# Per-category linear layer on one Trainium2 core: the categories taken in rotated order, their first weights and x loaded without the sort

## The reference

```python
selected_W = W[cat_ids]
selected_b = b[cat_ids]
x = x + jnp.einsum('bti,bio->bto', x, selected_W) + selected_b[:, None, :]
```

## Time and profile before

| what | value |
|---|---|
| three timed runs, median (lowest to highest) | 371.77 us (371.27 to 372.38) |
| profiled execution, first to last instruction | 371.0 us |
| PE busy | 356.9 us, 96% |
| POOL busy | 271.0 us, 73% |
| DVE, ACT busy | 172.1 us, 152.6 us |
| moved by DMA | 109.56 MB, mean 295 GB/s |

### The profile page before, as it was taken

One profiled execution on the slowest core, in us unless ns is written; L12 is line 12 of the kernel. 1 busy time (PEld: TensorE's weight loads), 2 busy tenths in 40 slices (PEclk: granted clock), 3 DMA queues, 4 the chain that ended last, 5 costly groups with the idle time before them and its releaser, 6 DMA issues.

```text
span 371.0 us, 6865 instructions
## 1 busy us (share of the span) xinstructions
PE 356.9 (96%) x1570; PEld 295.3 (80%) x1570; DVE 172.1 (46%) x271; ACT 152.6 (41%) x261; POOL 271.0 (73%) x145
## 2 busy tenths in 40 slices
PE   2969999999999999999999999999999999999996
PEld 2848888888888888888888888888888888888884
DVE  3534454454544545444454444545445454454542
ACT  4343245353544434343344525434542435453410
POOL 4299989678574688879893998989898889945000
PEclk9999999999999999999999999999999999999999
DMA  3979998999978799888998799989998999966622
GB/s 120 301 292 332 343 386 307 304 317 324 333 263 302 265 356 306 307 304 315 377 322 295 229 366 357 313 304 334 386 313 293 320 364 323 327 214 200 198 108 92
DMA packets 43379, 109.56 MB, mean 295 GB/s; under 512 B 4944, under 2 KB 5072, under 8 KB 38352
## 3 DMA queue, kind: packets, MB, share of 16 engines
q1 hardware_dynamic: 37296, 69.29, 52.7%
q0 software_dynamic: 5328, 38.80, 30.6%
q10 hardware_dynamic: 720, 1.05, 0.8%
HBM read 75.56 MB, written 33.55 MB: 294 GB/s over the span
## 4 chain that ended last, share of the span: by engine, by line
PE 92%; DMA 5%; DVE 1%; SPq 1%; issue 0%; DVEq 0%
PE pA L302 92%; DMA bb<-bias 4%; DMA idi<-ids 1%; SPq L132 0%; DVE os L275 0%; DVE xl L260 0%; PE pA L282 0%; SPq L117 0%; SPq L138 0%; DVE key L237 0%; DVE hot L241 0%; DVE cmp L239 0%; DVE rank L240 0%; DVE tb L244 0%; DVE idi L235 0%
## 5 line engine op out<-in xcount | busy, mean ns | idle before, releaser
L275 DVE TENSOR_TENSOR os<-pA,bb 128x512 f32<-128x512 f32 x128 | 88.7, 693 | 187.0 <-PE pA L302 178.7
L199 POOL TENSOR_TENSOR wl<-wr,wh 128x2048 fp32r<-128x2048 f32 x31 | 143.2, 4620 | 2.6
L302 PE MATMUL pA<-wh,xl 128*128 x512 | 137.7, 391 | 3.8 <-DVE xl L260 3.8
L302 PE MATMUL pA<-wl,xh 128*128 x512 | 137.7, 391 | 0.0
L302 PE MATMUL pA<-wh,xh 128*128 x512 | 137.1, 390 | 0.0
L219 ACT ACTIVATE pT<-xs 128x512 f32<-128x512 f32 x128 | 76.6, 598 | 110.9 <-DMA xs<-xt 105.1
L222 ACT ACTIVATE xh<-xs 128x512 fp32r<-128x512 f32 x128 | 80.4, 628 | 88.8 <-PE pA L302 88.4
L302 PEld LDWEIGHTS pA<-wh,xl 128*128 128x128 f32 x512 | 96.2, 188 | 24.3 <-issue 4.4
L302 PEld LDWEIGHTS pA<-wl,xh 128*128 128x128 f32 x512 | 96.7, 189 | 20.2
L302 PEld LDWEIGHTS pA<-wh,xh 128*128 128x128 f32 x512 | 96.4, 188 | 20.1
L195 POOL TENSOR_SCALAR wh<-wr 128x2048 fp32r<-128x2048 f32 x31 | 59.6, 1921 | 44.4 <-PE pA L302 38.6
(11 more groups left out here) (30 smaller groups left out, 14.1 us busy)
## 6 DMA issues: line engine op xcount, KB each, us to landing
xs<-xt SPq DMA_DIRECT2D x128, 256.0 KB, 5.4
out<-os SPq DMA_DIRECT2D x128, 256.0 KB, 4.9
wr<-w POOLq DMA_DIRECT2D x30, 1024.0 KB, 7.7
bb<-bias POOLq DMA_DIRECT2D x7, 1024.0 KB, 9.7
wr<-w ACTq DMA_DIRECT2D x4, 256.0 KB, 4.9
wr<-w SPq DMA_DIRECT2D x1, 1024.0 KB, 8.5
bb<-bias SPq DMA_DIRECT2D x1, 1024.0 KB, 13.1
idi<-ids SPq DMA_DIRECT2D x1, 64.0 KB, 3.8
```

The costliest lines, as they stand in the source:

```text
L199: eng.tensor_tensor(wl[:, at], wr[:, c % NR, :], wh[:, at].bitcast(f32), ALU.subtract).then_inc(s_w, 1)
L275: eng.tensor_tensor(os[:, i % NO, :], pA[i % NA][:, :], bb[:, bass.ds(at, D)], ALU.add).then_inc(s_fin, 1)
L302: mm = eng.matmul(pA[i % NA][:, :], xp[:, i % NH, k, :], wp[:, bass.ds(at + k * D, D)], start=(n == k == 0), stop=(n == 2 and k == KT - 1))
```

## The change

- **Order.** The categories are still taken in ascending order, but begin with that of element 0 and wrap around (`rot = (id - id[0]) & 31` in the sort key). Here the order becomes 21, 22, ..., 30, 31, 0, ..., 20, with 5, 5, 4, 3, 1, 5, 6, 2, 5, 6, 0, 6, 3, 9, 4, 3, 6, ... elements. So element 0 always comes first, and x of it is loaded at once, on ACT's queue.
- **First weights.** SP, ACT and POOL each read `ids[0]` from DRAM into a register (`category()`) and compute from it the address of every load of weights. SP issues the four chunks of c0, ACT issues c1 between its third and fourth conversion, POOL the rest.
- **Sort.** The ids come as one row on one partition; two matmuls spread it over the partitions and turn it into columns.
- **First batch elements.** PE works on element 0 chunk by chunk as the pieces of `wh`, `wl` come. c1 is prepared by ACT (`wh`), POOL and DVE (half of `wl` each).
- **Bias.** A group of four categories is read at the rotated place, from a bias array that the host writes twice in a row. The first row is loaded alone, the next three behind c1's identity step, and the other groups are issued by POOL in the middle of the preparation of their first category, where they stood beside the weights' load before.
- **End.** The last element's output is added and stored in two pieces, of 384 columns by SP and 128 by ACT.
- In ACT's and DVE's loops `xh` comes ahead of `pT`, the x load waits for `pT`, and PE waits for `xh` and `xl` apart.

```diff
+        def category(eng, name):
+            first = eng.alloc_register(f"{name}0")
+            eng.load(first, ids.rearrange("(a n) -> a n", a=1)[0:1, 0:1])
+            eng.reg_alu(first, first, C - 1, ALU.bitwise_and)
...
         @block.sync
-            eng.dma_start(idi[:, 0:128], ids.rearrange("(a n) -> a n", a=1).to_broadcast([128, 128])).then_inc(s_id, 16)
+            cat = category(eng, "sc")
+            c = cat(0)
+            for k in range(KT):
+                eng.dma_start(raw(0, k, k + 1), W[bass.ds(c, 1), :, k * D:(k + 1) * D].rearrange("a p d -> (a p) d"))\
+                   .then_inc(s_w0[k], 16)
             eng.wait_ge(s_tab, 1)
...
-                if i == 2:
-                    eng.dma_start(wr[:, 1, :], W[1, :, :]).then_inc(s_w1, 16)
-                if i == 3:
-                    bias_load(eng, 0)
...
         @block.gpsimd
-            def load(c):
-                eng.dma_start(wr[:, c % NR, :], W[c, :, :]).then_inc(s_wr[c % NR], 16)
-                if c % NB == 0:
-                    bias_load(eng, c // NB)
+            bias_load(eng, c0, 0, 1, s_b0)
+            eng.wait_ge(s_w1, 16)
+            eye = diagonal(1, 0, KT)
+            eng.tensor_tensor(eye, eye, ident[:, :, :], ALU.add).then_inc(s_ri, 1)
+            bias_load(eng, c0, 1, NB, s_bb[0])
+            eng.wait_ge(s_rh, KT)
+            eng.wait_ge(s_wd, 3)
+            eng.wait_ge(s_wp, 1)
+            load(2)
+            eng.wait_ge(s_rh, KT + 1)
+            eng.tensor_tensor(wl[:, chunk(1, 0, 2)], raw(1, 0, 2), wh[:, chunk(1, 0, 2)].bitcast(f32),
+                              ALU.subtract).then_inc(s_wp, 1)
+            eng.wait_ge(s_wp, 2)
+            eng.wait_ge(s_wd, 4)
+            eng.wait_ge(s_bb[0], 16)
+            eng.sem_inc(s_w, 1)
+            load(3)
+            for c in range(2, C):
+                eng.wait_ge(s_wr[c % NR], 16 * (c // NR))
+                eye = diagonal(c, 0, KT)
+                eng.tensor_tensor(eye, eye, ident[:, :, :], ALU.add).then_inc(s_ri, 1)
+                if c % NB == 0:
+                    bias_load(eng, c0, c, c + NB, s_bb[c // NB])
...
                 eng.tensor_scalar(wh[:, at], wr[:, c % NR, :], 1.0, 1.0, ALU.mult, ALU.mult).then_inc(s_wh, 1)
+                eng.wait_ge(s_wh, c - 1)
                 if c % NB == 0:
                     eng.wait_ge(s_bb[c // NB], 16)
...
         @block.scalar
+                if k == 2:
+                    eng.dma_start(wr[:, 1, :], W[bass.ds(cat(1), 1), :, :].rearrange("a p d -> (a p) d"))\
+                       .then_inc(s_w1, 16)
...
+                if i == 4:
+                    eng.wait_ge(s_ri, KT + 1)
+                    for k in range(0, KT, 2):
+                        eng.activation(wh[:, chunk(1, k, k + 2)], raw(1, k, k + 2), ACT.Copy).then_inc(s_rh, 1)
...
         @block.vector
+                for d0, d1 in ([(0, LAST), (LAST, D)] if i == B - 1 else [(0, D)]):
```

More of the change, by code:

```diff
@@ L173, in _ @@
                 eng.tensor_tensor(eye, eye, ident[:, 0:1, :], ALU.add).then_inc(s_ri, 1)
[L174 to L177, removed]
-            eng.sem_inc(s_w, 1)
[L179 to L185, removed]
+            eng.wait_ge(s_rh, 3)
@@ L243, in _ @@
             eng.wait_ge(s_bat, 1)
[L244 to L256, removed]
+            eng.tensor_copy(tb[:, :], pA[1][0:1, 0:128]).then_inc(s_tab, 1)
@@ L266, in _ @@
+            row = table(eng, "bo", tv, B, 0, (C - 1) * D)
             for i in range(B):
@@ L290, in _, with warm @@
-            eng.wait_ge(s_tab, 4)
-            eng.sem_inc(s_mm, 1)
-            row = table(eng, "wo", tc.rearrange("p n k -> p (n k)"), B, [1, 0], [C, (NW - 1) * KT * D])
-            for i in range(B):
-                c, at = row(i)
+            def warm(n):
+                for _ in range(n):
+                    eng.matmul(pA[0][:, 0:128], ones[:, :], ones[:, :], start=True, stop=True)
+            eng.wait_ge(s_one, 1)
+            eng.sem_inc(s_mm, 1)
+            warm(7)
+            eng.wait_ge(s_row, 2)
@@ new lines, in _ @@
+            warm(2)
+            HH, HL, LH = 0, 1, 2
+            first = [(HH, 0), (HH, 1), (LH, 0), (LH, 1), (HL, 0), (HH, 2), (LH, 2), (HL, 1),
+                     (HH, 3), (LH, 3), (HL, 2), (HL, 3)]
+            early = [(p, k) for p in (HH, HL, LH) for k in range(KT)]
+            plain = [(p, k) for p in (LH, HL, HH) for k in range(KT)]
+            pair = {HH: (xh, wh), HL: (xh, wl), LH: (xl, wh)}
+            eng.wait_ge(s_xh, 1)
+            for n, (p, k) in enumerate(first):
+                if p == HH:
+                    eng.wait_ge(s_rh, k + 1)
+                if (p, k) == (LH, 0):
+                    eng.wait_ge(s_xl, 1)
+                if p == HL and k == 2:
+                    eng.wait_ge(s_wp, 1)
+                elif p == HL:
+                    eng.wait_ge(s_wd, (1, 2, 0, 3)[k])
+                xp, wp = pair[p]
+                mm = eng.matmul(pA[0][:, :], xp[:, 0, k, :], wp[:, chunk(0, k, k + 1)],
+                                start=(n == 0), stop=(n == 3 * KT - 1))
@@ new lines, in _ @@
+            mm.then_inc(s_mm, 1)
+            eng.wait_ge(s_hot, 2)
+            eng.matmul(pS[0:1, 0:C], ones[:, 0:1], below[:, :], start=True, stop=True).then_inc(s_bat, 1)
+            eng.wait_ge(s_tab, 2)
+            row = table(eng, "wo", tc, B, 1, C)
+            at_reg = eng.alloc_register("at")
+            row(0)
+            for i in range(1, B):
+                c = row(i)
+                eng.reg_alu(at_reg, c, NW - 1, ALU.bitwise_and)
+                eng.reg_alu(at_reg, at_reg, WS, ALU.mult)
+                at = eng.snap(at_reg, min_val=0, max_val=(NW - 1) * WS)
```

216 lines of the change are left out of this document (137 added, 79 removed).

## The result

The changed kernel takes 375.61 us in the median (373.91 to 379.06, 4 runs) against 371.8 before, a ratio of 1.0132 with a 95% interval of 1.007 to 1.0194. The kernel is slower; 372.0 with a range of 369.0 to 375.5 was forecast.

What follows compares the result with a forecast made beforehand. PE's unbroken run bounds the kernel; after the change POOL's chain readies c5 at 67.1. Adding 1.7 for the clock and 299.2 for 110 elements gives 368.0; tail 3.4 - 0.2 gives 371.2, frame 0.8 gives 372.0 us; range 369.0 to 375.5.

Steps and rivals of the forecast that it cites:

- c1's weights there: ACT's load of c1, issued at 9.0 on its own queue, lands after 5.9 us, at 14.9.
- PE at the end of element 17: PE ends 18 elements at 60.5: element 0 near 12, 17 x 2.72 us, and 2.3 for waits.
- For 1.75 MB instead of 2 that is 10.4 x 0.875 = 9.1: c2's weights are there at 25.3: POOL issues three bias rows, then c2's weights, at 16.2; the pair was taken to land in 9.1 us.
- 0.3 for the address arithmetic on POOL: At the end of POOL's chain to c5, address work adds 0.3 us once: 66.8 becomes 67.1.
- c3's 9.1: POOL's preparation of c3 takes 9.1 us, so c3 is ready at 42.4.
- the 10.4 taken: c5's weights and c4's bias group on POOL's queue need 10.4 us from the first issue; third pass starts at 53.1.
- The clock: Half clock on PE behind the stop in front of element 18 costs 1.7 us, between 0 and twice that.
- The frame: The timed median lies 0.8 us above the profiled execution's span, so 371.2 becomes 372.0.
- The tail: The split of the last output changes the 3.4 us tail by -0.2 us (-0.5 to +0.3).
- The bias wait: c4's third pass on POOL waits for its bias group, worth 5.6 us; c4 is ready at 57.7.
- The id load: SP's two dependent loads of the id from DRAM take 2.8 us; c0's first chunk is issued at 3.6.
- Later categories aren't late again: Behind c5 PE doesn't stop for POOL: c8 is ready 33.7 us after c5, PE comes to it after 37.1.
- The bias is hidden: Rival: bias lands within about 2.9 us of issue, c5 ready at 61.5, time 365.5 us; chance 0.14.

Runs made afterwards that it cites:

- the cured kernel: Changed kernel's control with bias groups from c4 on issued by POOL right behind their first category's weights, as before the change: 368.5 us, ratio 0.9956.
- fixed addresses, bias early: Kernel with bias groups issued beside the weights, given constant addresses in POOL's weight loads: 369.44 us, ratio 0.9959.
- the control: Changed kernel with one more register operation (a mask with 255) ahead of PE's and POOL's waits on table values: 375.06 us, ratio 1.0123.
- The fixed addresses: Changed kernel with the extra register operation, POOL's weight loads (c2 to c31) given constant instead of computed addresses, bias still late: 374.6 us, ratio 1.0117.
- the order from 0: Changed kernel with the extra register operation, rotation begun at element 7's category, 0, bias still late: 381.99 us, ratio 1.0294.
- control of before: Kernel before the change with one extra register operation ahead of the waits on table values: 369.98 us, ratio 0.9979.
- before with late bias: Kernel before, with the extra register operation, bias groups from c4 on moved between identity step and second pass: 372.62 us, ratio 1.0041.
- address ahead: Kernel with bias groups issued beside the weights; POOL computes the load address two categories on before waiting for its third pass: 367.96 us, ratio 0.9941.
- category 0 first, bias early: Changed kernel with the extra register operation, rotation begun at category 0 and bias groups issued beside the weights' loads: 369.02 us, ratio 0.9954.

## Why the prediction was wrong

The mechanism was the forecast's. There is one long stop in front of element 18, released by POOL's third pass of c5; POOL waits for the bias inside c4; half clock follows; c8 is no stop. The forecast was that this loss would about cancel the won time, 372.0 against 371.8; it was larger, and 375.6 lies 0.1 us outside the range. Wrong were sizes, nearly all to one side. (The prediction's "second passes of c2 and c5" that end at 35.25 and 63.56 are the third ones, L199, and it is the third pass that waits for the bias; the numbers are right.) Against the sum:

| term | forecast | measured |
|---|---|---|
| c1's weights there | 14.9 | 14.3 |
| c2's weights there | 25.3 | 26.2 |
| c2, c3 ready | 33.3, 42.4 | 34.2, 43.7 |
| c4, c5 ready | 57.7, 67.1 | 59.3, 68.8 |
| PE at the end of element 17 | 60.5 | 62.5 |
| clock behind the stop | 1.7 | 2.3 |
| tail | 3.2 | 3.5 |
| around the span | 0.8 | 1.5 |

The forecast misses the profiled execution by 3.6 us: 1.7 in c5, 0.1 until PE goes on, 0.6 in the clock, 0.2 in the run, 0.3 in the tail and 0.7 around the span.

- **The step that failed most** is "For 1.75 MB instead of 2 that is 10.4 x 0.875 = 9.1: c2's weights are there at 25.3". From the bias's issue at 15.58 to the weights' landing at 26.16 the pair took 10.6 us, 1.5 more; POOL's earlier start (15.58 and not 16.2) hid 0.6 of it, so c2's weights came 0.9 later. In this execution the landing did not follow the bytes. It isn't a constant either: the same pair took 9.7 us in the cured kernel and 9.9 with its fixed addresses, and in the control c2 started at 24.36 and didn't wait for its weights. There POOL stood 1.93 us for DVE's half of c1's `wl`, ahead of c3's load, a gate that the sum leaves out.
- **The second** is "0.3 for the address arithmetic on POOL". It is 0.5 us for each of three categories, 1.5 in all. No row showed such an operation on POOL, and I gave it no upper bound. The fixed addresses show the term (0.80 to 0.30). Of these 1.2 us too little, 0.8 show at c5. The rest was luck: c3's 9.1 was 0.1 too much for a category that waits for no slot, the pair in c4 landed 0.3 sooner than the 10.4 taken, and c5's third pass was 0.1 shorter.
- *The clock* cost 2.3 us and not the 1.7 of the earlier trace rows.
- *The frame.* The span of 371.0 was held against a median of 371.8. In later runs with both numbers the kernel before lies 1.8 us above its span (370.11 against 368.3) and the changed one 1.5. So the profiled execution of before was about 1 us slower than the median, and the 0.8 came from two different executions. Its mean clock is 0.995; in the later runs of that kernel the executions with such a clock are the slower ones (last section).
- *The tail.* From the last output add's start to the end it was 3.3 us before (371.0 - 367.72) and is 3.4 here (374.1 - 370.69). No gain of the split shows; -0.2 was forecast. (Its 192 KB less are 0.67 us at the mean rate, not 0.5.)
- *The bias wait* was sized well: c4 took 59.3 - 43.7 = 15.6 us, forecast 15.3, and the third pass waited 5.5 us. By the rule of the Trainium skill ("DMA: Bandwidth & Descriptors", the anatomy of one DMA on the SWDGE path; 4.4 us for 1 MB is an estimate from its figures) the wait would have been 1.5 us. The load took 8.2 us from its issue, so this trace speaks against using that rule behind another load and in traffic.
- *The id load* cost less than the 2.8 taken: SP's two loads took 0.84 + 0.47 = 1.3 us, and its four chunks go out at 2.50 and not at 3.6.

The step "Later categories aren't late again" was right of the time but too easy. It counted c8 and waved at the rest. In the changed kernel POOL keeps almost no lead behind c5 (0.6 us of waits for PE), and in the order from 0 it holds PE up twice, late in the program. Of the rivals, "The bias is hidden" gives the time of the cured kernel: 5.6 to 6.5 us less than the forecast was its account (366.4 to 365.5 against 372.0), and 6.2 less than the control were measured.

## What to carry to other kernels

Count the lead of a helper engine over the bottleneck not only at the start but as a rate: here 9.1 us a category against 10.9, which one late DMA in four categories and half a microsecond of address work used up. A DMA that a pass needs belongs a whole stage ahead of it. When a stop is gone from a profile, look at both sides of it: the helper may have become quicker, or the bottleneck may have come later. Time won at the start is worth nothing behind the first point at which another chain is later.

## What the runs showed of the hardware

- A load of a register from DRAM isn't one price. SP took 0.84 and 0.47 us for the two dependent loads; ACT and POOL, who did the same a microsecond later and at the same time, took 1.6 to 1.8 each. Why isn't shown:

```profile
L122 SPq TENSOR_LOAD <-ids_ptr x1: 840/840/840, 0.9 to 0.9; - x1
L122 SPq TENSOR_LOAD <-ids x1: 469/469/469, 1.7 to 1.7; - x1
...
L122 POOLq TENSOR_LOAD <-ids_ptr x1: 1617/1617/1617, 2.0 to 2.0; - x1
...
L122 POOLq TENSOR_LOAD <-ids x1: 1833/1833/1833, 3.7 to 3.7; - x1
```

- PE's clock doesn't fall behind every stop, and the length of the stop alone doesn't say when. Behind stops of 1.36 us (cured kernel), 2.60 (control of before) and 2.74 (before with late bias) the next four matmuls took 1.17 to 1.20 us. Behind 1.55 (address ahead), 2.28 (fixed addresses, bias early), 2.50 (category 0 first, bias early), 3.49, 4.90 and 6.46 us the granted clock went to the lower level for a while, and PE lost 1.6 to 2.3 us. The control of before:

```profile
25.06 1.17 PE L313 MATMUL pA<-wh,xl 128*128 x4 [2.60 <-DVE xl L270]
```

and the kernel with the address ahead, where the granted clock was 1.00 from 12 to 15 us, 0.67 from 15 to 17 and 0.50 from 17 to 19:

```profile
15.19 1.65 PE L431 MATMUL pA<-wh,xh 128*128 x4 [1.55 <-ACT xh L280]
```

- The granted clock goes with the slow end of the kernel before. Of its 81 executions beside the experiments, 51 have a mean clock of 0.999 or 1.000 and took 366.65 to 371.34 us; the other 30 have 0.994 or 0.995 and took 371.36 to 372.93. The execution that the earlier trace rows are read from has 0.995. What spreads the 51 over 4.7 us isn't shown.
